# Moving ScalarE's copies for the degree table behind 16 more groups of gathers in a graph-network kernel

## The chip, the cores and the metric

The kernel runs on one core of one Trainium2 chip. The metric is device microseconds of one launch, as the median of several runs. Beside the runs there is one profiled execution, whose time and span are given below. Start times in the trace are microseconds from the start of the span.

## The reference

The inputs are x (100,000 nodes x 128 features), 25,000 edges (src, dst), and edge_attr (25,000 x 64). What is computed:

```
h = relu(layernorm(x))
two layers of:  fwd = segment_mean(h[src] over dst); bwd = segment_mean(h[dst] over src)
                h = concat(h, fwd, bwd) @ W + b        (relu after the first layer only)
x = x + h
h = relu(layernorm(x))
agg = segment_sum(edge_attr over dst)
x = x + MLP(concat(h, agg, u[0]))                      (256 -> 256 -> 256 -> 128, leaky relu)
```

The segment means divide by the degrees of the nodes (how often a node stands in dst, or in src, and at least 1). The part of the kernel around the change prepares those degrees.

## The kernel before

The edges are worked on in G = 98 groups of 256. Each group has 512 edge ends (4 slots of 128 partitions). Each engine has a program of its own; they meet only at semaphores, and within an engine the order is that of the text. The program has these parts, one after the other:

- **The first stage.** Two jobs run side by side. The first is the *picks*: for each group g, ScalarE writes two index columns (`pick_at`, L748) and issues the zero fill of a later piece of `sums1` (512 KB, L741, only up to g = 93); GpSimd then issues two indirect gathers of rows of x into `picked` (L589); SyncE stores `picked` to `xdst` (L376). `picked` and `pick_at` have four buffers each. The second is the *count* of degrees: VectorE writes one-hot rows (`onehot_lo` L980, `onehot_hi` L981, 392 instructions of each), and TensorE multiplies them (L1301, two matmuls for each pair of one-hots) into four banks of PSUM. The two jobs share no data.
- **The degree table.** When the count has ended, VectorE copies the banks to `degree` (L1099), TensorE transposes them (L1392) and signals `s_degT` twice. ScalarE then copies the banks to the high half of `table` (`degree_table()`, L756 and L757, twice) and signals `s_tablehi`; VectorE writes the low half (L1104, L1106) and signals `s_table`. TensorE waits for `s_table` before everything of layer 1: `spread_keys` (L1338), `look_up` (28 matmuls, L1319), `degrees` (L1330), the transposes (L1346) and products (L1355, L1361).
- **The first two groups of layer 1.** VectorE's program goes on, after the table, with `upper_digits(1)`, `lower_digits(0)` (L1043, needs the look-up), `repeated(0)` (L1052 to L1060), `end_stats` and `negated` of groups 0 and 1 (L996, L1005, L1010), `scales(0)`. ScalarE's side of this is `first_group()`: `centre(0)`, `centre(1)` (L685, L691), `transposed(0)` (L701), `messages(0)` (L711), `dense_rows(0)` (L722).
- **The loop of layer 1** over the groups. Its scatters into `sums1` (L579, four for each group) are GpSimd's. Then layer 2 and the MLP, which the change doesn't touch.

The order of the picks is the same on SyncE, GpSimd and ScalarE. It is written in `picks(eng, pick, early, late, last)`: groups 0 to 3; a loop over groups 4 to 59; `early()`; a loop over 60 to 75; `late()`; a loop over 76 to 91; `last()`; groups 92 to 97. With `early`, SyncE and GpSimd load the first two groups of layer 1 (`first_loads`, `first_ends`). With `last`, SyncE loads and GpSimd gathers group 2, and ScalarE does `first_group()`. Only ScalarE uses `late`:

```
picks(act, pick, nothing, degree_table, first_group)
```

Of the kernel before, what the change touches and what calls it, by code (L numbers as in the profile page):

```python
# [29 lines left out]
def gnn_kernel(nc, x, src, dst, edge_attr, W1, b1, W2, b2, u, w1, b1m, w2, b2m, w3, b3, out):  # L30
# [34 lines left out]
    with ExitStack() as ctx:  # L65
# [217 lines left out]
        def picks(eng, pick, early, late, last):  # L283


            for g in range(4):
                pick(g, g, 1)
            with eng.Fori(1, EARLY) as q:
                for b in range(4):
                    pick(q * 4 + b, b, q + 1)  # L290
            early()
            with eng.Fori(EARLY, LATE) as q:
                for b in range(4):
                    pick(q * 4 + b, b, q + 1)
            late()
            with eng.Fori(LATE, QUADS - 1) as q:
                for b in range(4):
                    pick(q * 4 + b, b, q + 1)
            last()
            for g in range(4 * QUADS - 4, G):  # L300
                pick(g, g % 4, g // 4 + 1)
# [4 lines left out]
        def hold(eng):  # L306


            eng.sem_inc(passed[eng.engine], 1)

        def before(g, n):

            return not isinstance(g, int) or g >= n
# [359 lines left out]
        def _(act):  # L673
# [3 lines left out]
            def layer1():  # L677
                def src_index(g, b):

                    act.activation(index[:, b, 0:2], keys[:, 0, 2:4, bass.ds(g, 1)].rearrange("p s g -> p (s g)"), ACT.Copy)\  # L680
                        .then_inc(b_index, 1)

                def centre(g, b, uses):
                    act.wait_ge(b_moments, g + 1)
                    act.activation(spread[:, b, :], moments[:, b, :, 1], ACT.Sqrt, bias=eps[:, 0:1]).then_inc(b_spread, 1)  # L685
                    act.wait_ge(b_negmean, g + 1)
                    if before(g, 2):

                        act.wait_ge(b_T, g - 1)
                    for s in range(4):  # L690
                        last = act.activation(normed[:, b, s, :], ends[:, b, s, :], ACT.Identity, bias=negmean[:, b, s:s + 1])  # L691
                    last.then_inc(b_centred, 1)
                    if not isinstance(g, int) or g + 2 < G:

                        act.wait_ge(b_src[b], 32 * uses)
                        hold(act)
                        src_index(g + 2, b)

                def transposed(g, b):
                    act.wait_ge(b_T, g + 1)  # L700
                    act.activation(hT[:, b].rearrange("p s f -> p (s f)"), bank[0][:], ACT.Relu).then_inc(b_hT, 1)  # L701

                def messages(g, b):
                    act.wait_ge(b_prod, g + 1)
                    act.wait_ge(b_scale, g + 1)
                    if before(g, 2):

                        act.wait_ge(b_mm, g - 1)
                    hold(act)
                    for s in range(4):  # L710
                        last = act.activation(group_msg[:, b, s, 0:F], bank[1][:, s * P:(s + 1) * P], ACT.Copy,  # L711
                                              scale=endscale[:, b, s:s + 1])
                    last.then_inc(b_msg, 1)

                def dense_rows(g, b, uses):
                    act.wait_ge(b_ymm, g + 1)
                    if before(g, 2):

                        act.wait_ge(b_ykept[b], 16 * (uses - 1))
                    hold(act)  # L720
                    for s in range(4):
                        last = act.activation(end_dense[:, b, (s + 2) % 4, :], bank[5][:, s * P:(s + 1) * P], ACT.Copy,  # L722
                                              scale=rstd[:, b, s:s + 1])
                    last.then_inc(b_yrows, 1)
# [15 lines left out]
                def fill(rows_of, n):  # L740
                    act.dma_start(rows_of.rearrange("(p r) f -> p r f", p=P),  # L741
                                  zeros[:, 0:n * F].rearrange("p (r f) -> p r f", f=F)).then_inc(s_zeroed, 16)
# [10 lines left out]
                def degree_table():  # L753
                    for c in range(2):
                        act.wait_ge(s_degT, c + 1)
                        act.activation(table[:, c, 0, 0:4, :], bank[4 + 2 * c][0:CW, :].rearrange("p (c f) -> p c f", f=P), ACT.Copy)  # L756
                        act.activation(table[:, c, 0, 4:CH, :],  # L757
                                       bank[5 + 2 * c][0:CW, 0:(CH - 4) * P].rearrange("p (c f) -> p c f", f=P), ACT.Copy)\
                            .then_inc(s_tablehi, 1)

                def first_group():
                    centre(0, 0, 1)
                    centre(1, 1, 1)
                    transposed(0, 0)
                    messages(0, 0)
                    dense_rows(0, 0, 1)
# [6 lines left out]
                act.wait_ge(s_eps, 1)  # L773
                for g in range(2):
                    src_index(g, g)
                picks(act, pick, nothing, degree_table, first_group)
                fill(sums1[G * FILL:NR, :], GS // P)
                sweep(act, G // 2, lambda j: [step(j * 2 + b, b, j + 1) for b in range(2)])

            layer1()  # L780
            act.wait_ge(s_bias, 48)

# [831 lines left out]
```

## Time and profile before

| what | value |
|---|---|
| median of 3 runs | 4322.13 us (4296.8, 4322.13, 4326.12) |
| profiled execution, its own time | 4294.77 us |
| its span | 4293.2 us |
| mean granted TensorE clock | 0.944 of full |
| busy share of the span | PE 87%, DVE 74%, POOL 70%, ACT 54% |

The profiled execution's time is 1.6 us over its span. It belongs with the lowest of the three runs, 27 us (0.6%) under their median. The first stage and the entry into layer 1 take the first 440 us or so of the span, and the loop of layer 1 goes on to about 1446 us.

### The profile page before, as it was taken

How to read it: one execution, taken by the hardware profiler on the slowest of the kernel's cores; microseconds unless marked ns; L12 is line 12 of the kernel's file. 1: busy time of each engine (PE TensorE's matmuls, PEld its weight loads, DVE VectorE, ACT ScalarE, POOL GpSimd, SP SyncE). 2: the span in 40 equal slices, each digit the busy share in tenths (PEclk: the TensorE clock that was granted, in tenths of full speed). 3: DMA queues.
4: the chain of work that ended last, by engine and by line, in shares of the span. 5: the costliest groups of instructions: out<-in, count | busy, mean ns of one | idle time of the engine just before them, and what ended most of it. 6: DMA issues, size and time to landing. Idle time of an engine off the chain costs nothing.

```text
span 4293.2 us, 100093 instructions
## 1 busy us (share of the span) xinstructions
PE 3733.9 (87%) x25698; PEld 3280.8 (76%) x25698; DVE 3181.9 (74%) x11005; ACT 2304.9 (54%) x5788; POOL 2999.4 (70%) x2962
## 2 busy tenths in 40 slices
PE   3485899988988688888888888879999999999999
PEld 0123788887888688878788888868888888888888
DVE  2384788888888555556555555569999999999998
ACT  0001444444444455555555555557777777777776
POOL 6614778788888677777777777766666666666665
PEclk6687999999999899999999999989999999999999
DMA  7815777777777577777777777767777777777775
GB/s 277 288 52 169 174 176 176 178 176 176 180 176 180 132 188 190 182 186 190 190 190 190 178 183 189 179 147 158 158 159 157 159 158 158 160 157 158 159 159 123
DMA packets 818323, 742.05 MB, mean 173 GB/s; under 512 B 200444, under 2 KB 629896, under 8 KB 818282
## 3 DMA queue, kind: packets, MB, share of 16 engines
q1 hardware_dynamic: 637702, 522.72, 41.2%
q0 software_dynamic: 166208, 167.10, 26.8%
q10 hardware_dynamic: 14372, 51.75, 3.1%
q8 instruction: 17, 0.28, 0.0%
q14 instruction: 24, 0.20, 0.0%
HBM read 355.07 MB, written 334.83 MB: 161 GB/s over the span
## 4 chain that ended last, share of the span: by engine, by line
PE 40%; DMA 7%; issue 6%; DVE 4%; another core or an unknown queue 3%; ACT 2%; POOL 2%; SPq 2%; ACTq 0%; DVEq 0%; POOLq 0%
PE bank L1559 8%; DMA normed<-in_x_dram 6%; PE bank L1573 4%; PE bank L1572 4%; PE bank L1574 4%; PE bank L1537 2%; PE bank L1530 2%; PE bank L1531 2%; PE bank L1536 2%; PE bank L1532 2%; PE bank L1546 2%; PE bank L1467 2%; DVE stats L1160 2%; PE bank L1468 1%
## 5 line engine op out<-in xcount | busy, mean ns | idle before, releaser
L626 POOL DMA_INDIRECT node<-summed,rep_index x392 | 625.9, 1597 | 229.3 <-issue 147.8
L579 POOL DMA_INDIRECT sums<-summed,rep_index x392 | 620.4, 1583 | 156.5 <-issue 130.2
L657 POOL TENSOR_TENSOR resid<-node_out,b3s 128x128 f32<-128x128 f32 x784 | 336.4, 460 | 478.1 <-DVE rows L1281 475.3
L1231 DVE SCALAR_TENSOR_TENSOR z<-bank,bias,small 128x512 f32<-128x512 f32 x784 | 567.7, 744 | 68.3 <-ACT small L889 59.2
L889 ACT ACTIVATE small<-bank,bias_small 128x512 f32<-128x512 f32 x784 | 535.0, 683 | 107.1 <-PE bank L1574 59.5
L667 POOL TENSOR_TENSOR z_lo<-z,z_hi 128x512 fp32r<-128x512 f32 x392 | 496.5, 1288 | 10.2 <-ACT z_hi L920 10.2
L611 POOL DMA_INDIRECT ends<-sums,index x392 | 381.8, 974 | 121.7 <-issue 120.2
L1467 PE MATMUL bank<-hx,W1s 128*128 128x128 f32 x1568 | 324.9, 291 | 159.8 <-ACT hx L830 151.7
L1467 PEld LDWEIGHTS bank<-hx,W1s 128*128 128x128 f32 x1568 | 251.2, 201 | 193.1 <-issue 192.8
L1559 PE MATMUL bank<-w3s,z 128*128 128x128 f32 x3136 | 382.4, 275 | 3.1 <-DVE z L1231 3.1
L1559 PEld LDWEIGHTS bank<-w3s,z 128*128 128x128 f32 x3136 | 365.7, 192 | 4.0 <-DVE z L1231 4.0
L589 POOL DMA_INDIRECT picked<-in_x_dram,pick_at x196 | 188.1, 960 | 216.2 <-ACT pick_at L748 128.0
L1319 PE MATMUL bank<-upper,table 112*128 112x256 bf16 x2744 | 322.3, 276 | 16.8 <-DVE upper L1035 8.7
L820 ACT ACTIVATE resid<-normed,shift,rstd 128x128 f32<-128x128 f32 x784 | 323.1, 498 | 1.6 <-DVE shift L1176 1.1
L809 ACT ACTIVATE spread<-moments,eps 128x4 f32<-128x4 f32 x196 | 58.2, 297 | 494.9 <-DVE moments L1165 245.6
L1301 PE MATMUL bank<-onehot_hi,onehot_lo 128*128 128x392 bf16 x784 | 196.7, 382 | 144.8 <-issue 82.7
L1572 PE MATMUL bank<-z_hi,w_hi 128*128 128x512 f32 x784 | 322.1, 411 | 0.0
L1468 PE MATMUL bank<-ident,rows 128*128 128x128 f32 x1568 | 318.3, 286 | 0.0
L1319 PEld LDWEIGHTS bank<-upper,table 112*128 112x128 bf16 x2744 | 267.7, 99 | 55.7 <-DVE upper L1035 13.3
L1444 PE MATMUL bank<-group_msg,same 128*128 128x192 f32 (+1 forms) x1960 | 308.7, 313 | 0.0
L1573 PE MATMUL bank<-z_lo,w_hi 128*128 128x512 f32 x784 | 306.1, 390 | 0.0
L1574 PE MATMUL bank<-z_hi,w_lo 128*128 128x512 f32 x784 | 305.8, 390 | 0.0
(152 smaller groups left out, 9762.6 us busy)
## 6 DMA issues: line engine op xcount, KB each, us to landing
node<-blank SPq DMA_DIRECT2D x98, 768.0 KB
sums<-zeros ACTq DMA_DIRECT2D x98, 512.0 KB
normed<-in_x_dram SPq DMA_DIRECT2D x196, 256.0 KB
rows<-sums SPq DMA_DIRECT2D x196, 256.0 KB
y<-node_out SPq DMA_DIRECT2D x196, 256.0 KB
node_out<-node SPq DMA_DIRECT2D x196, 256.0 KB, 3.2
node_out<-y POOLq DMA_DIRECT2D x196, 256.0 KB, 4.2
a_parts<-a_pair SPq DMA_DIRECT2D x784, 64.0 KB, 2.5
```

The source lines that it names most:

```text
L579: pool.indirect_dma_start(sums1, bass.IndirectOffsetOnAxis(ap=rep_index[:, b, s:s + 1], axis=0), summed[:, b, s, 0:F], None, compute_op=AL ...
L611: pool.indirect_dma_start(ends[:, b, s, :], None, sums1, bass.IndirectOffsetOnAxis(ap=index[:, b, s:s + 1], axis=0))\
L626: pool.indirect_dma_start(node1, bass.IndirectOffsetOnAxis(ap=rep_index[:, b, s:s + 1], axis=0), summed[:, b, s, :], None, compute_op=ALU. ...
L667: pool.tensor_tensor(z1_lo[:, st.b % 2, m, :], z1[:, st.b % 2, m, :], z1_hi[:, st.b % 2, m, :].bitcast(F32), ALU.subtract).then_inc(e_z1lo, 1)
L889: act.activation(small[:, m, :], bank[first_bank + m][:], ACT.Identity, scale=SLOPE, bias=bias_small[:, m:m + 1]).then_inc(ready, 1)
L1231: dve.scalar_tensor_tensor(out=z[:, m, :], in0=bank[first_bank + m][:], scalar=bias[:, m:m + 1], in1=small[:, m, :], op0=ALU.add, op1=ALU. ...
L1319: last = pe.matmul(bank[2][:, c * EG:(c + 1) * EG], table[:, c, i, r, :], upper[:, b, r, c * EG:(c + 1) * EG], start=(r + i == 0), stop=(r ...
L1467: pe.matmul(o, W1s[:, 0, :], hx[:, i, s, :], start=True, stop=False)
L1559: last = pe.matmul(bank[4][:, s * P:(s + 1) * P], z2[:, c, s * P:(s + 1) * P], w3s[:, c, :], start=(c == 0), stop=(c == HB - 1))
L1572: pe.matmul(bank[2 + m][:], w2_hi[:, c, cols], z1_hi[:, d, c, :], start=(c == 0), stop=False)
L1573: pe.matmul(bank[2 + m][:], w2_hi[:, c, cols], z1_lo[:, d, c, :], start=False, stop=False)
L1574: last = pe.matmul(bank[2 + m][:], w2_lo[:, c, cols], z1_hi[:, d, c, :], start=False, stop=(c == HB - 1))
```

## The change

`degree_table()` is taken from the place `late`, behind group 75, and put at the head of `first_group()`, behind group 91. Nothing else is touched, on any engine.

```
                 def first_group():
+                    degree_table()
                     centre(0, 0, 1)
                     centre(1, 1, 1)
                     transposed(0, 0)
...
-                picks(act, pick, nothing, degree_table, first_group)
+                picks(act, pick, nothing, nothing, first_group)
```

`degree_table()` is two waits and four instructions:

```
for c in range(2):
    act.wait_ge(s_degT, c + 1)
    act.activation(table[:, c, 0, 0:4, :], bank[4 + 2 * c]...)
    act.activation(table[:, c, 0, 4:CH, :], bank[5 + 2 * c]...).then_inc(s_tablehi, 1)
```

## Rows read from the trace of the kernel before

**Rows 1.** The page, busy tenths of GpSimd in 40 slices of 107 us.
```profile
POOL 6614778788888677777777777766666666666665
```

**Rows 2.** Busy time in stretches: PE, PEld, DVE, ACT, POOL, TensorE clock, DMA share, GB/s.
```profile
14.00:238.00 224.00, 85.91 (x272) 25.75 (x272) 69.70 (x264) 14.72 (x72) 148.93 (x156) 0.62 0.78 277
238.00:349.50 111.50, 110.78 (x512) 30.40 (x512) 110.11 (x512) 0.00 (x0) 0.00 (x0) 0.98 0.01 3
349.50:398.00 48.50, 17.51 (x89) 12.69 (x89) 17.28 (x62) 9.74 (x34) 30.44 (x32) 0.60 0.71 251
```

**Rows 3.** The same view for line L981 alone, VectorE's `onehot_hi`.
```profile
20.00:40.00 20.00, 5.94 (x19) 0.88 0.86 322
40.00:60.00 20.00, 1.89 (x6) 0.50 0.72 251
...
20.00:238.00 218.00, 45.28 (x132) 0.61 0.78 275
238.00:349.50 111.50, 84.46 (x256) 0.98 0.01 3
```

**Rows 4.** The same view for line L589 alone, GpSimd's pick gathers.
```profile
20.00:238.00 218.00, 138.90 (x145) 0.61 0.78 275
...
349.50:398.00 48.50, 30.44 (x32) 0.60 0.71 251
```

**Rows 5.** Timeline of ScalarE: start, us, what, and the idle time before it.
```profile
351.67 0.60 ACT L756 ACTIVATE table<-bank 112x512 bf16<-112x512 f32 x1 [122.11 <-PE bank L1392]
...
392.00 1.28 ACT L685 ACT_TABLE_LOAD   x1 [0.46 <-issue]
...
396.21 0.57 ACT L701 ACTIVATE hT<-bank 128x512 f32<-128x512 f32 x1
402.50 1.14 ACT L711 ACTIVATE group_msg<-bank,endscale 128x128 f32<-128x128 f32 x4 [5.71 <-remote]
...
404.02 0.67 ACT L722 ACTIVATE end_dense<-bank,rstd 128x128 f32<-128x128 f32 x2
```

**Rows 6.** Timeline of GpSimd.
```profile
236.38 0.95 POOL L589 DMA_INDIRECT picked<-in_x_dram,pick_at  x1 [0.30 <-issue]
354.48 0.95 POOL L589 DMA_INDIRECT picked<-in_x_dram,pick_at  x1 [117.15 <-ACT pick_at L748]
...
405.57 0.95 POOL L589 DMA_INDIRECT picked<-in_x_dram,pick_at  x1 [5.28 <-issue]
...
423.18 1.63 POOL L579 DMA_INDIRECT sums<-summed,rep_index  x1 [0.31 <-issue]
```

**Rows 7.** Timeline of VectorE.
```profile
69.67 0.29 DVE L980 TENSOR_SCALAR onehot_lo<-iota_lo,hilo 128x256 bf16<-128x256 f16 x1 [4.39 <-remote]
...
364.42 0.75 DVE L1043 SCALAR_TENSOR_TENSOR lower<-hilo_all,digits,bank 128x512 f32<-128x512 f16 x1 [6.11 <-remote]
...
368.67 0.87 DVE L996 BATCH_NORM_STATS2 stats<-ends 128x6 f32<-128x128 f32 x4
...
379.95 0.17 DVE L1010 TENSOR_SCALAR negmean<-moments 128x4 f32<-128x4 f32 x1 [0.96 <-DVE moments L1005]
...
407.07 0.87 DVE L996 BATCH_NORM_STATS2 stats<-ends 128x6 f32<-128x128 f32 x4 [11.79 <-DMA ends<-xdst]
...
408.54 0.17 DVE L1010 TENSOR_SCALAR negmean<-moments 128x4 f32<-128x4 f32 x1
...
434.08 0.75 DVE L1043 SCALAR_TENSOR_TENSOR lower<-hilo_all,digits,bank 128x512 f32<-128x512 f16 x1 [18.57 <-remote]
```

**Rows 8.** Timeline of TensorE.
```profile
348.76 0.76 PE L1301 MATMUL bank<-onehot_hi,onehot_lo 128*128 128x392 bf16 x3
...
355.78 4.89 PE L1319 MATMUL bank<-upper,table 112*128 112x256 bf16 x28
...
396.84 2.08 PE L1355 MATMUL bank<-W1s,hT 128*128 128x128 f32 x8 [0.91 <-issue]
```

**Rows 9.** Line L579, GpSimd's scatters of layer 1: shortest, median, longest ns, first and last start.
```profile
L579 POOL DMA_INDIRECT sums<-summed,rep_index x392: 1550/1577/1680, 423.2 to 1444.4; - x196
```

More of the change, by code:

```diff
@@ L761, in first_group @@
                 def first_group():
+                    degree_table()
                     centre(0, 0, 1)
@@ L775, in layer1 @@
                     src_index(g, g)
-                picks(act, pick, nothing, degree_table, first_group)
+                picks(act, pick, nothing, nothing, first_group)
                 fill(sums1[G * FILL:NR, :], GS // P)
```

## The prediction

> **What bounds the kernel now.** I read the page's slices first: GpSimd is 6 tenths busy in slices 1 and 2, 1 tenth in slice 3 (215 to 322 us), and busy again from slice 4 on [rows 1]. So something in the first stage stops the picks. The timelines say what: ScalarE stood for 122.1 us until TensorE's transposes of the degrees, and GpSimd for 117.2 us until ScalarE's next `pick_at` [rows 5, 6]. The last gather before the stop ends at 237.3 and the next starts at 354.5. ScalarE was at `degree_table()` with nothing to copy, and the 16 groups of picks behind it had no need of the table. Read so far, the change looks like 40 us for nothing.
>
> The view by stretches is the one that decides. The reader is to compare its first two rows [rows 2]. While the picks run (14 to 238 us), DMA is 78% busy, the granted clock averages 0.62 of full, and VectorE and TensorE, which only count and share no data with the picks, are busy 31% and 38% of the time. When the picks have stopped (238 to 349.5), DMA is at 1%, the clock at 0.98, and both are busy 99%. The same for `onehot_hi` alone: 132 in 218 us beside the picks, 0.606 each us; 256 in 111.5 us without them, one each 0.4355 us, 2.296 each us [rows 3]. So the stall of GpSimd is time in which the count runs at nearly four times its speed. The end of the count (349.5, the last matmuls of L1301 [rows 8]) releases the table, the table releases the entry into layer 1, and the loop of layer 1 then runs to 1446 us, paced by its own work: its 392 scatters start over 1021 us, 10.4 us a group [rows 9], of which four of 1.58 us and the 0.3 us behind each are 7.5, and GpSimd's two gathers of group rows come on top. No idle time waits there to take up a later or earlier start. So the price of the change is by how much the point is moved at which that loop gets going; everything behind it moves along.
>
> **The change, part by part.** I measure at the end of `dense_rows(0)`, the last instruction of `first_group()`, 404.02 + 0.67 = 404.7 [rows 5], which is 55.2 us behind the end of the count. Behind it the programs of both kernels are the same. It is (end of the count) + (chain from there).
>
> *1. The four copies themselves.* The same four instructions, some 0.6 us each at most [rows 5], leave one place and enter another. They release VectorE directly in both. Cost 0.
>
> *2. What the copies no longer hold up: 16 groups of picks.* These are 16 `pick_at`, 16 zero fills of 512 KB, 32 gathers on GpSimd and 16 stores on SyncE. They now run from 237 us on, where the stall stood. Gathers of groups up to 75 came 145 in 218 us, 3.01 us a group [rows 4], so the 16 groups take 48.1 us at that pace; behind the count they took from 354.5 to about 397.8, or 43 us, 32 gathers [rows 4, 6]. I take 48.1, since it is the pace beside a running count, and keep 43 as the other end. The picks end at some 285 us, far ahead of the count's end, so ScalarE reaches `degree_table()` with 100 us to spare and the table isn't made late by its new place. SyncE's and GpSimd's `last` steps get a free queue.
>
> *3. What that costs the count.* In 48.1 us beside picks VectorE writes 48.1 x 0.606 = 29.1 of `onehot_hi`, which alone take 29.1 x 0.4355 = 12.7 us. The count ends 48.1 - 12.7 = 35.4 us later, at 384.9. With 43 us of picks it is 26.1 counted, 11.4 us saved, 31.7 later. Single stretches of 20 us beside picks held 6 to 19 of `onehot_hi` [rows 3], so over 48 us, where such stretches partly even out, I allow 31 to 40 us. The bounds from further off: 48 us, if the count stood altogether, and 0, if the picks weren't what slowed it.
>
> *4. The chain from the end of the count to `dense_rows(0)`.* In the kernel before it shares the DMAs with the 16 groups and ScalarE serves it only behind them: `centre(0)` starts, with a table load, at 392.0, 0.5 us behind the last `pick_at` of group 91, although `negmean` of group 1 had been ready since 380.1 [rows 5, 7]. On the way VectorE waits 6.1 us for `lower`, which starts 3.7 us behind the last matmul of the look-up (355.78 + 4.89 = 360.7) [rows 7, 8]. Without picks I add up: end of the count to the start of the look-up 6.3 (349.5 to 355.8); the look-up 4.9; from `lower` to `stats` 4.25 (364.42 to 368.67); `stats` to the end of `negmean` twice, 2 x 1.64 (407.07 to 408.71); the second `centre` behind it 1.5 (392.0 to 396.2 held the load of 1.3 and two of them); `hT` 0.6; its products 2.1 and the second half of them as much; `dense_rows` 1.2 [rows 5, 7, 8]. That is 26.2, and 27.2 with hand-overs of 0.1 us or so each. ScalarE's table load of 1.28 us before the first square root finds room while VectorE does group 1. Against the 55.2 of before the chain gains 28.0 us. The other end: if the waits inside the chain stay (380.1 - 349.5 = 30.6 to `negmean`, then 12.7 from 392.0 to 404.7 less the first centre, 1.4), it is 42, and gains 13. I take 27.2, for those waits stood in the stretch with DMA at 0.71, and rows 2 show VectorE without gaps where DMA is idle.
>
> *5. Behind `dense_rows(0)`.* Groups 92 to 97 are picked, GpSimd issues 12 gathers and two more from 405.57 and then the first scatter at 423.18 [rows 6]; VectorE's `lower` of group 2 waits 18.6 us until 434.1 [rows 7], and the loop is at speed from about 440. The same traffic meets the same steps in both kernels, only the backlog of groups 88 to 91 is gone. I take 2 us for it; bounds are 0 and 10 us of gain (the part of the 18.6 us that lies behind GpSimd's queue).
>
> *The sum:* + 35.4 - 28.0 - 2 = + 5.4 us. Against the profiled execution 4294.8 becomes 4300.2; against the median of the runs, 4322.1, it is 4327.5. The profiled execution stands with the lowest run, and runs of the same kernel lie up to 29 us apart, five times the effect. About 1% (43 us) is what a measurement of this kernel can tell from no change.
>
> **A rule of the Trainium skill.** VectorE waited 4.4 us ahead of a one-hot (69.67 us) while single gathers take 0.95 us on GpSimd [rows 6, 7]. The Trainium skill, "SBUF — State Buffer", says that VectorE in a two-port mode and GpSimd take a shared pair of ports by an exclusive lock, held for one instruction. By that rule the count would lose only GpSimd's busy time, 32 x 0.95 = 30.4 us, and the sum would be + 0.4 us instead of + 5.4. The trace speaks against it as the whole cause, as the wait is longer than several such instructions and 0.3 us lie free between them.
>
> **The rivals.**
>
> *A. The count isn't slowed by picks* (it was slow by its own start, with TensorE's clock at the lower level). Then item 3 is 0, and the time is 4322.1 - 28 - 2 = 4292. For it: the granted clock in the first stretch is 0.62 [rows 2]. Against it: VectorE is idle two thirds of it too, and the full rate stands from 238.0, 0.7 us behind the last gather's end, not from a point of the count's own. Chance 0.06.
>
> *B. The picks cost the count less than the average.* 43 us of picks, 19 of `onehot_hi` in each 20 us (the best stretch), the 10 us behind: 43 - 17.8 = 25 us later, - 28 - 10 = - 13, 4309. The port rule above goes this way too, with + 0.4. Chance 0.12 for gains of 6 to 20 us.
>
> *C. The chain doesn't shorten.* The waits of VectorE and ScalarE between the count and `dense_rows(0)` belong to their entering new code and not to the traffic. Place: `lower` and `negmean` on VectorE, `group_msg` on ScalarE. Then the chain is 42 and the sum 35.4 - 13 - 2 = + 20, 4342; with the count standing still beside the picks, + 33, 4355. It decides from a chain of some 34 us behind the count on, where the sum passes + 12. For it: they are marked as ended by an unknown queue. Against: in the stretch without DMA no such wait stands. Chance 0.14.
>
> *D. The change does nothing* (ScalarE would stand elsewhere for the same 122 us, and the picks with it): the program's order excludes it, since nothing between groups 76 and 91 needs the table. Below 0.01.
>
> **How the numbers follow.** The forecast, - 6 to + 15 us about + 5, has 0.67; A 0.06; B 0.12; C 0.14; D and the rest 0.01. The range takes in B and C and the spread of the runs: the low end is 4297 (the lowest run) + 5 - 13 = 4289, the high end 4326 + 20 = 4346. Faster by over 1% would need under 4279: only A together with low runs, 0.02. Slower by over 1% is over 4365: C with a count that stands still and high runs, 0.03. Within 1%: 0.95.
>
> **What would show it.** In the profile of the changed kernel: GpSimd's gathers run on without a gap from 237 to about 285 us; `onehot_hi` there some 29 in 48 us with the clock near 0.6; the last L1301 at 385 and not at 349.5; ScalarE's wait ahead of `table` about 100 us, now behind group 91; from the last count matmul to `lower` 12 us rather than 15, to the end of `dense_rows(0)` 27 rather than 55; first scatter at some 427 to 430 rather than 423.2; scatters still 10.4 us a group. I'm wrong if the count's end stays below 370 (then A or B) or if the chain behind it is over 34 us (C).

## The result

| kernel | runs | median | lowest to highest |
|---|---|---|---|
| before | 12 | 4318.75 us | 4282.96 to 4336.83 |
| changed | 12 | 4322.24 us | 4253.59 to 4326.57 |

The changed kernel's runs fall into two groups with nothing between them: five at 4253.59, 4262.65, 4263.43, 4265.45 and 4269.83, and seven from 4322.10 to 4326.57. The ratio 0.9879 [0.9842, 0.9916] counts the upper seven as slow runs and leaves them out; the changed kernel's profile on another chip (a_again, below) runs as I forecast and speaks for their being the kernel itself (forecast 4327.5), though no run of this upper group was profiled. The lower group is something that I hadn't forecast. The profiled execution, 4262.65 us with a span of 4261.0, is of the lower group.

The page of the changed kernel has GpSimd's slices, for [rows 1]: the hole of slice 3 is gone, a shallow one of 311 to 345 us is left in slice 4.
```profile
POOL 6674877887777677777777777766666666666665
```
The view by stretches, for [rows 2]: PE, PEld, DVE, ACT, POOL busy, granted clock, DMA share, GB/s.
```profile
180.00:200.00 20.00, 4.18 (x10) 0.66 (x10) 2.52 (x9) 1.02 (x5) 15.60 (x17) 0.50 0.57 191
217.00:311.00 94.00, 93.97 (x441) 24.96 (x440) 94.00 (x441) 4.91 (x24) 77.26 (x55) 1.00 0.61 210
```
This is the reading that decides. The second row can't be had by mixing rows 2 of before: GpSimd is 82% busy with picks, DMA is at 0.61, and VectorE and TensorE are 100% busy with the clock at 1.00. In the row above it, which ends 17 us earlier, the same two jobs share the chip at the old price: 9 VectorE instructions in 20 us. The same view for `onehot_hi` alone (now L982, since lines behind the added one moved by one), for [rows 3]:
```profile
20.00:238.00 218.00, 59.19 (x181) 0.65 0.74 261
238.00:290.00 52.00, 37.40 (x123) 1.00 0.66 228
```
Where I had forecast 0.606 each us beside the picks of groups 76 to 91, it was 123 / 52 = 2.37. From here on I call such a way for the two jobs to share the chip, with its own pair of rates, a regime: slow for 0.6 of `onehot_hi` each us, fast for 2.3 and more. The timeline of GpSimd shows where the one gives way to the other, for [rows 6]:
```profile
200.51 0.95 POOL L589 DMA_INDIRECT picked<-in_x_dram,pick_at  x1 [0.30 <-issue]
215.84 1.11 POOL L589 DMA_INDIRECT picked<-in_x_dram,pick_at  x1 [14.38 <-DMA xdst<-picked]
...
309.57 1.41 POOL L589 DMA_INDIRECT picked<-in_x_dram,pick_at  x1 [0.30 <-issue]
...
369.23 1.63 POOL L579 DMA_INDIRECT sums<-summed,rep_index  x1 [0.30 <-issue]
```
At about 201 us GpSimd waits 14.38 us for a store of `picked`, which stands on SyncE's queue behind `first_loads` (group 60, `early`). Up to there a gather takes 0.95 us, behind it 1.41. The gathers go on without a stop from 237 us, as forecast, but to 311 and not to 285. The timelines of TensorE, VectorE and ScalarE give the chain, for [rows 5, 7, 8]:
```profile
321.69 5.46 PE L1302 MATMUL bank<-onehot_hi,onehot_lo 128*128 128x392 bf16 x25
...
333.42 3.22 PE L1320 MATMUL bank<-upper,table 112*128 112x256 bf16 x28
```
```profile
336.68 0.75 DVE L1044 SCALAR_TENSOR_TENSOR lower<-hilo_all,digits,bank 128x512 f32<-128x512 f16 x1 [0.99 <-PE bank L1320]
...
343.89 0.17 DVE L1011 TENSOR_SCALAR negmean<-moments 128x4 f32<-128x4 f32 x1
...
380.37 0.75 DVE L1044 SCALAR_TENSOR_TENSOR lower<-hilo_all,digits,bank 128x512 f32<-128x512 f16 x1 [22.03 <-remote]
```
```profile
329.30 0.60 ACT L756 ACTIVATE table<-bank 112x512 bf16<-112x512 f32 x1 [28.92 <-PE bank L1393]
...
331.24 1.28 ACT L685 ACT_TABLE_LOAD   x1
...
348.22 1.14 ACT L711 ACTIVATE group_msg<-bank,endscale 128x128 f32<-128x128 f32 x4 [2.28 <-PE bank L1356]
...
350.38 0.38 ACT L722 ACTIVATE end_dense<-bank,rstd 128x128 f32<-128x128 f32 x1
```
The count ends at 321.69 + 5.46 = 327.15 (before: 349.52), 22.4 us earlier, and `dense_rows(0)` at 350.76 (404.7), 53.9 us earlier. From the one to the other it is 23.6 us instead of 55.2. The first scatter follows 18.5 us behind, as in before: 369.2 instead of 423.2.

Grouped rows of the scatters of layer 1 and, in the second, of layer 2 (shortest, median, longest ns, first and last start), for [rows 9]:
```profile
L579 POOL DMA_INDIRECT sums<-summed,rep_index x392: 1549/1577/1690, 369.2 to 1397.9; - x196
L626 POOL DMA_INDIRECT node<-summed,rep_index x392: 1549/1577/2141, 1430.3 to 2772.1; - x196
```
The kernel before, the second of them:
```profile
L626 POOL DMA_INDIRECT node<-summed,rep_index x392: 1550/1577/2161, 1477.7 to 2803.2; - x196
```
So 54.0 us at the first scatter, 46.5 at the last, 31.1 at the end of layer 2, and 32.2 in the span. It looks like a gain given back. It isn't shown to be one: see "The rest of the span" below.

### The profile page after: what moved, and what is told of

It is laid out like the page before. It is cut to its first block, busy times and chain, and to the rows that moved or that the text cites. A ratio compares the mean times of both kernels' runs of the same rounds, so it can differ in the third digit from the quotient of the medians.

```text
span 4261.0 us, 100093 instructions
## 1 busy us (share of the span) xinstructions
PE 3726.9 (87%) x25698; PEld 3278.0 (77%) x25698; DVE 3177.7 (75%) x11005; ACT 2305.6 (54%) x5788; POOL 3023.1 (71%) x2962
## 4 chain that ended last, share of the span: by engine, by line
PE 41%; issue 7%; DMA 6%; DVE 4%; another core or an unknown queue 4%; ACT 3%; SPq 1%; POOL 1%; ACTq 0%; DVEq 0%; POOLq 0%
PE bank L1560 8%; DMA normed<-in_x_dram 5%; PE bank L1574 4%; PE bank L1573 4%; PE bank L1575 4%; PE bank L1538 2%; PE bank L1531 2%; PE bank L1532 2%; PE bank L1537 2%; PE bank L1533 2%; PE bank L1547 2%; DVE stats L1161 2%; PE bank L1468 2%; PE bank L1469 1%
## 5 line engine op out<-in xcount | busy, mean ns | idle before, releaser
L579 POOL DMA_INDIRECT sums<-summed,rep_index x392 | 620.0, 1582 | 164.6 <-issue 131.1
L1445 PEld LDWEIGHTS bank<-group_msg,same 128*128 128x128 f32 x1960 | 299.6, 192 | 0.0
```

The source lines that it names most:

```text
L579: pool.indirect_dma_start(sums1, bass.IndirectOffsetOnAxis(ap=rep_index[:, b, s:s + 1], axis=0), summed[:, b, s, 0:F], None, compute_op=AL ...
L1445: last = pe.matmul(o, same[:, b, j, i * P:(i + 1) * P], group_msg[:, b, j, 0:w], start=(j == 0), stop=(j == i))
```

## The experiments

Four sets ran, each on another chip. The kernel before took 4051.2, 4286.6, 4317.5 and 4316.3 us on them (medians of 13, 23, 15 and 13 runs), so every kernel is compared with before on its own chip. e1, e2, e3, e5 and e6 are edits of the changed kernel, e4 is one of the kernel before; a is the changed kernel and b the kernel before, without an edit.

| run | chip of | median (runs) | before there | ratio | last matmul of the count starts | first scatter |
|---|---|---|---|---|---|---|
| e1_loads_last | set 1 | 4072.57 (8) | 4051.22 | 1.0079 [1.0052, 1.0106] | 201.1 | 310.7 |
| e2_fills_after | set 1 | 4180.10 (2) | 4051.22 | 1.0320 [1.0295, 1.0345] | 190.5 | 414.9 |
| e3_head_start | set 1 | 4117.41 (5) | 4051.22 | 1.0163 [1.0149, 1.0178] | 187.5 | 358.6 |
| e4_head_start_late | set 1 | 4103.35 (4) | 4051.22 | 1.0133 [1.0115, 1.0151] | 188.8 | 343.0 |
| a_again | set 2 | 4292.34 (12) | 4286.58 | 0.9983 [0.9945, 1.0022] | 383.8 | 426.3 |
| b_again | set 2 | 4283.05 (8) | 4286.58 | 0.9997 [0.9963, 1.0031] | 352.9 | 426.5 |
| e5_one_port | set 2 | 4371.83 (2) | 4286.58 | 1.0196 [1.0112, 1.0280] | 272.2 | 537.9 |
| e1_again | set 3 | 4323.45 (10) | 4317.45 | 1.0006 [0.9987, 1.0025] | 387.4 | 431.7 |
| e2_again | set 3 | 4440.93 (1) | 4317.45 | one run | 399.3 | 567.2 |
| e3_again | set 3 | 4347.70 (4) | 4317.45 | 1.0069 [1.0043, 1.0095] | 187.8 | 455.6 |
| e4_again | set 3 | 4295.83 (6) | 4317.45 | 0.9856 [0.9822, 0.9891] for its lower three | 187.2 | 450.1 |
| a_third | set 4 | 4315.74 (10) | 4316.34 | 0.9981 [0.9947, 1.0015] | 329.7 | 374.9 |
| b_third | set 4 | 4323.23 (1) | 4316.34 | one run | 357.3 | 435.4 |
| e6_psum_rows | set 4 | 4429.58 (2) | 4316.34 | 1.0270 [1.0230, 1.0310] | 501.4 | 545.0 |

The theories, as the expectations name them: R, the regime changes by itself, whatever the loads do; Q, the DMA queues are overfull while the count is slow, and a pause in them lets the count get to speed; P, VectorE and GpSimd share a way to memory, and who has it keeps it; T, turns of about 0.7 us that hold instruction streams while GpSimd gathers, whatever the one-hot looks like.

**Set 1: four edits, on a chip where nothing of this stands in the way.** The first moves the loads of groups 0 and 1 from `early` to `last`, so that no pause falls among the picks:
```
-picks(sp, pick, first_loads, nothing, lambda: loads(2, 0, 2))
+picks(sp, pick, nothing, nothing, lambda: (first_loads(), loads(2, 0, 2)))
-picks(pool, pick, first_ends, nothing, lambda: gather_src(2, 0))
+picks(pool, pick, nothing, nothing, lambda: (first_ends(), gather_src(2, 0)))
```


> The changed kernel, with the loads for the first two groups of layer 1 (first_loads on SyncE, first_ends on GpSimd) moved from behind group 59 to behind group 91, so that nothing pauses the picks in the middle. Theory Q (two regimes: the count runs slowly while the picks keep the DMA queues overfull, and a pause of the picks of 14 us lets it change to full speed, which it then keeps beside the picks): without the pause no change of regime; onehot_hi stays near 0.6 each us until the picks end at some 285 us, the count ends at some 385, the first scatter starts at some 430, median within 10 us of 4322. Theory R (the full speed beside picks comes from the change itself or from the time since the start, not from the pause): the count again runs at 2.3 each us from some 210 us on and ends near 328, time near 4262.

The second takes the zero fills out of the picks, behind the whole first stage:
```
-if not isinstance(g, int) or g + 4 < G:
-    fill(sums1[bass.ds((g + 4) * FILL, FILL), :], FILL // P)
...
 picks(act, pick, nothing, nothing, first_group)
+with act.Fori(4, G) as g:
+    fill(sums1[bass.ds(g * FILL, FILL), :], FILL // P)
```


> The changed kernel with the zero fills of groups 4 to 97 (512 KB each) taken out of the picks and issued in one loop behind the last pick; GpSimd's first scatter waits for all of them, so the whole gets longer by 100 to 160 us. Only the first 330 us of its profile are of interest. Theory Q (DMA queues overfull): with some 512 KB of 900 KB a group gone, the count runs at 2.3 onehot_hi each us beside the picks from the start and ends at 185 to 200 us; gathers take 1.40 us each until then, 0.95 behind it. Theory P (the port shared by VectorE and GpSimd alone): the gathers are still there, 0.95 us long, and the count stays at some 0.6 each us beside them.

The third lets the count run alone until 48 of its matmul pairs are done, and the fourth does the same to the kernel before:
```
+pool.wait_ge(s_count, 48)
 picks(pool, pick, first_ends, nothing, lambda: gather_src(2, 0))
```


> The changed kernel, with GpSimd's first pick gather held back until the first 48 of 392 count steps are done (some 22 us of picks lost), so that the picks meet a count that already runs at full speed with TensorE's clock up. Theory Q: the fast regime holds from the start: gathers 1.40 us, 3.4 us a group, onehot_hi 2.3 each us, count ended at 185 to 200 us; the picks of group 91 end at 310 to 330, then the table and its chain of 21 to 27 us; first scatter at 355 to 380; all runs close together, at 4245 to 4275. Theory R: the count falls to 0.6 each us as soon as gathers start, and all is 10 to 20 us later than in the changed kernel, two groups of times as there.

> The same head start of 48 count steps in the kernel before, whose table copies stand behind group 75. Theory Q: the count has ended (at 185 to 200 us) before ScalarE comes to the copies (at 260 to 280 us), so neither ScalarE nor the picks wait there, the chain behind the table runs beside the last picks, first_group() follows the pick of group 91 at 310 to 330 at once; first scatter at 335 to 355, 15 to 25 us ahead of the head start in the changed kernel; time 4225 to 4260. Theory R: as the kernel before, 10 to 20 us later.

These runs tell little between the theories, because on this chip the count was never slow. By stretches, e1_loads_last:
```profile
40.00:180.00 140.00, 136.92 (x606) 34.34 (x606) 140.00 (x607) 10.43 (x51) 109.37 (x101) 1.00 0.81 282
```
DMA is at 0.81, higher than in [rows 2], GpSimd is 78% busy with gathers, and VectorE has no gap. The count is over at 201 us, when the picks are still running. Copies at their old place don't stop the picks on such a chip: in e4_head_start_late ScalarE reached them at 272.98 us and waited 0.47 us. What these runs show is the price of the edits where there is nothing to win. Against before it is 21 us for e1, 129 for e2 and 66 for e3, each together with the move of the copies, since the changed kernel itself didn't run on this chip, and 52 for e4, which has the head start alone. The pair e3 and e4 differs by the move alone: with it the kernel is 14 us slower (4117.41 against 4103.35, first scatter 358.6 against 343.0). In this pair, where the count is over early, the move costs. That the same kernel before takes 4051 us here and 4287 to 4318 on the other three chips is the largest difference of this study, and it isn't explained.

**Set 2: the two kernels again.** No edit.

> The changed kernel once more. On a chip where the kernel before takes some 4050 us, theory Q: the count is over before either place of the copies, so nothing is freed by the move, and the chain of table, look-up and statistics (21 us in the first profile after, 26.2 added up in the prediction) now lies behind the pick of group 91 instead of beside the picks: 10 to 25 us slower than before, ratio 1.003 to 1.006. On a chip where before takes some 4300 us: two groups of times, 4253 to 4270 and 4322 to 4327. Theory R: the move saves the 33 to 54 us of the first pair of profiles on either chip, ratio 0.987 to 0.992.

> The kernel before once more, for its profile beside runs of the other chip. On a chip where the kernel before takes some 4050 us, theory Q says that the count runs at full speed beside the picks from the start (2.2 onehot_hi each us), ends at some 200 us, and that ScalarE therefore doesn't wait at the copies behind group 75: first scatter at 290 to 300. On a chip where it takes some 4300 us: a stop of the picks of 60 to 120 us there, first scatter at 370 to 425. Theory R (nothing differs but the later parts): the stop is there on either chip.

The changed kernel, a_again, its 12 runs: one at 4231.82 and the others from 4279.60 to 4308.50, so all but one lie together, and the one some 48 us under them. Its profiled execution (4288.08) shows what I had forecast. `onehot_hi` by stretches, the last three at the pause of the picks behind group 59:
```profile
20.00:238.00 218.00, 43.73 (x135) 0.61 0.75 269
238.00:286.00 48.00, 9.92 (x30) 0.57 0.75 268
290.00:380.00 90.00, 66.19 (x209) 1.00 0.02 6
205.00:208.00 3.00, 2.02 (x7) 0.50 1.07 382
208.00:215.00 7.00, 4.88 (x16) 1.00 0.54 196
216.00:236.00 20.00, 1.61 (x5) 0.56 0.71 257
```
Its timelines of GpSimd, TensorE and ScalarE:
```profile
210.62 0.95 POOL L589 DMA_INDIRECT picked<-in_x_dram,pick_at  x1 [8.64 <-DMA xdst<-picked]
...
375.70 8.45 PE L1302 MATMUL bank<-onehot_hi,onehot_lo 128*128 128x392 bf16 x39
...
386.31 0.60 ACT L756 ACTIVATE table<-bank 112x512 bf16<-112x512 f32 x1 [103.01 <-PE bank L1393]
...
407.37 0.38 ACT L722 ACTIVATE end_dense<-bank,rstd 128x128 f32<-128x128 f32 x1
```
30 of `onehot_hi` in 48 us of picks (forecast 29.1), the count's end at 384.15 (384.9), ScalarE's wait 103 us (about 100), the chain 407.75 - 384.15 = 23.6 us (27.2), and the first scatter at 426.3 (427 to 430). Against before on the same chip, whose count ended at 353.27, that is 30.9 us later, at the lower end of my 31 to 40.

The pause at `early` was shorter here, 8.64 us, and the gathers behind it kept their 0.95 to 1.02 us. The three rows at the pause show two things more. The count was at full speed from 205 us on, and for 3 us of it the granted clock was still 0.50: so a lower clock of TensorE isn't what makes the slow regime slow. And it stayed at full speed for some 4 us beside the first gathers, with the clock at 1.00, and then fell to 5 of `onehot_hi` in 20 us. To be at full speed when the gathers come isn't enough to stay there. The kernel before on this chip, ScalarE's timeline:
```profile
355.42 0.60 ACT L756 ACTIVATE table<-bank 112x512 bf16<-112x512 f32 x1 [123.04 <-PE bank L1392]
```
and its first scatter at 426.5: the later count and the shorter chain cancel to 0.2 us. I had expected a stop of 60 to 120 us and a first scatter at 370 to 425 here; both came out a little above.

**Set 2: one-hots with another way of reading.** Each iota value is stored twice and read with step 2, so that VectorE might give up its fast form of reading:
```
-pool.iota(iota_hi[:], pattern=[[1, HALF]], ...)
+pool.iota(iota_hi[:], pattern=[[1, HALF], [0, 2]], ...)
...
-dve.tensor_scalar(onehot_hi[:, s, :], iota_hi[:], ...)
+dve.tensor_scalar(onehot_hi[:, s, :], iota_hi[:].rearrange("p (n t) -> p n t", t=2)[:, :, 0], ...)
```
(`iota_lo` likewise.)

> The changed kernel with the counting rows iota_lo and iota_hi stored with a step of 2 elements, so that VectorE's one-hots read with a step and run at one element a cycle: some 0.33 and 0.47 us in place of 0.20 and 0.23 from start to start, 0.8 us a pair, 310 us of count. Theory P (gathers and one-hots contend for what the fast form of the one-hots uses): gathers stay at 0.95 us throughout, and no waits of several us ahead of the one-hots anywhere; count ended at 325 to 345 us. Theory Q (DMA queues overfull, sequencers wait): on a chip of 4300 us the waits of 0.7 us and their multiples stay, with the count still at 0.6 each us beside the picks; on a chip of 4050 us no such waits in either case, and the gathers alone tell about the port (0.95 against 1.08 to 1.41).

The edit didn't do what it was for: a pair of one-hots takes 0.59 us from start to start (0.26 and 0.34), where I had expected 0.8 and the unedited pair takes 0.43. So this run doesn't test P. But its trace holds the clearest row of all. GpSimd:
```profile
53.20 219.59 POOL L589 DMA_INDIRECT picked<-in_x_dram,pick_at  x1 [6.14 <-ACT pick_at L748]
```
VectorE in the middle of it:
```profile
200.39 0.34 DVE L981 TENSOR_SCALAR onehot_lo<-iota_lo,hilo 128x256 bf16<-128x256 f16 x1
200.65 0.41 DVE L982 TENSOR_SCALAR onehot_hi<-iota_hi,hilo 128x392 bf16<-128x392 f16 x1
```
One gather of a usual 0.95 us took 219.59 us, and 368 pairs of one-hots without a gap ran beside it; the last of them ends at 271.97 and the gather at 272.79. So GpSimd can be kept out for as long as the one-hots come. No long pause stood ahead of it: the wait before this gather is 6.14 us, shorter than the one in a_again. Both of its runs were slower than before's median (4399.28 and 4344.39); whether by 2% or less is unclear.

**Set 3: the edits of set 1 where the count is slow.**

> The changed kernel with first_loads and first_ends moved behind group 91, once more, for a chip on which the kernel before takes some 4300 us. Theory Q (the count changes to full speed only if the picks pause long enough): as there is no pause, the profile shows 0.6 onehot_hi each us to some 285 us, a count ended at some 385 and a first scatter at 426 to 432; all runs in the upper group of the changed kernel's times, none 40 us under it. Theory R (the change of regime comes by itself): some runs 40 to 60 us under the others. On a chip of 4050 us: as in the first run, 4061 to 4102.

Without the loads at group 60 the count stayed slow until the picks ended. `onehot_hi` by stretches:
```profile
200.00:286.00 86.00, 15.81 (x49) 0.58 0.73 255
290.00:380.00 90.00, 79.94 (x202) 0.95 0.09 28
```
From 30 to 290 us GpSimd's longest wait is 4.12 us. The first scatter came at 431.7, and the ten runs lie between 4305.94 and 4327.72: no lower group. That is as Q expected and speaks against R, by which the regime would have changed without the pause, but weakly: where 8 runs in 34 of the unedited kernel lie low (below), ten without one come about 1 time in 15 by chance, and that kernel wasn't run on this chip.

> The changed kernel with the zero fills of groups 4 to 97 behind the last pick, once more, for a chip of 4300 us; the whole is 60 to 140 us longer, only the first 300 us count. Theory Q (DMA queues overfull): count at 2.3 onehot_hi each us from the start beside the gathers, ended at 185 to 200 us. Theory P (port alone): 0.6 each us beside the gathers.

By stretches, all engines:
```profile
20.00:200.00 180.00, 53.50 (x151) 11.22 (x148) 38.77 (x147) 12.47 (x61) 121.48 (x128) 0.55 0.35 103
```
The fills are gone and DMA is at 0.35 instead of 0.78, and yet VectorE is 22% busy, less than in [rows 2]. The theory of the overfull queues falls with this row, and with e1_loads_last from the other side (DMA at 0.81, count at full speed). What is left beside the count is the gathers, 128 in these 180 us. So they alone can bring the slow regime on such a chip, though on the chip of set 1 they don't.

> The changed kernel with the head start of 48 count steps, once more, for a chip of 4300 us. Theory Q: regime of full speed from the start and kept, as in the run on the other chip: gathers of 1.40 us, count ended at some 190 us, first scatter at 355 to 365; time 4225 to 4245, that is 65 us less the 10 us or so of GpSimd's later parts, under the upper group of the changed kernel's times. Theory R: the count falls to 0.6 each us when the gathers start, first scatter at 430 to 450.

> The kernel before with the head start of 48 count steps, once more, for a chip of 4300 us. Theory Q: first scatter at 343 as on the other chip, so 80 us ahead of the kernel before (423 to 426): 4200 to 4225, ratio 0.980 to 0.984 where the kernel before takes 4287. On a chip of 4050 us: again 50 us slower than before. Theory R: slower than before on either chip.

With a head start of 48 pairs the count kept full speed on this chip too, to its end at 188 us, and GpSimd paid: the first scatter came at 455.6 and 450.1, where 355 to 365 and 343 were expected, and e3_again took 4347.70 us and not 4225 to 4245. The gathers weren't at 1.40 us. e3_again by stretches, and its GpSimd:
```profile
40.00:180.00 140.00, 139.94 (x654) 37.11 (x654) 140.00 (x655) 2.46 (x12) 130.83 (x26) 1.00 0.19 68
```
```profile
41.56 26.00 POOL L589 DMA_INDIRECT picked<-in_x_dram,pick_at  x1 [34.55 <-PE bank L1303]
67.86 6.53 POOL L589 DMA_INDIRECT picked<-in_x_dram,pick_at  x1 [0.30 <-issue]
```
26 gathers in 140 us, 5 us each, the first 26.00 and the later ones down to some 3. The same kernel on the chip of set 1, the same stretch:
```profile
40.00:180.00 140.00, 139.94 (x656) 37.09 (x654) 140.00 (x656) 7.98 (x39) 113.58 (x81) 1.00 0.63 219
```
81 gathers of 1.4 us beside the same count. So three regimes exist, not one, and one kernel can meet more than one of them. The head start in the kernel before (e4_again) ran 4254.33, 4256.71 and 4259.94 in three runs and 4331.73, 4344.33 and 4354.37 in three. The ratio in the table describes the lower three alone. The profiled one (4331.73) is of the upper three, with gathers of up to 26 us; no trace of a lower one was taken.

**Set 4: once more, and one-hots that read from PSUM.**

> The changed kernel once more. On a chip of 4050 us (count fast beside the picks from the start): 10 to 25 us slower than before. On a chip of 4300 us: like before within 5 us, first scatter at 426 to 430, but single runs 40 to 60 us under the rest.

> The kernel before once more. On a chip of 4050 us: no stop of the picks at the copies, first scatter at 285 to 300. On a chip of 4300 us: stop of 115 to 125 us, first scatter at 423 to 427.

The changed kernel ran 4261.28 and 4265.81 in two runs and 4304.50 to 4329.71 in eight. The profiled one is of the lower two. Its GpSimd:
```profile
201.21 0.95 POOL L589 DMA_INDIRECT picked<-in_x_dram,pick_at  x1 [0.30 <-issue]
218.92 1.32 POOL L589 DMA_INDIRECT picked<-in_x_dram,pick_at  x1 [16.76 <-DMA xdst<-picked]
220.54 1.40 POOL L589 DMA_INDIRECT picked<-in_x_dram,pick_at  x1 [0.30 <-issue]
```
Its `onehot_hi`:
```profile
20.00:200.00 180.00, 32.06 (x99) 0.60 0.75 266
220.00:300.00 80.00, 58.05 (x188) 1.00 0.64 219
```
It is the picture of the first profile again: a pause of 16.76 us at the same place, 0.55 of `onehot_hi` each us ahead of it, 2.35 behind it, gathers 0.95 and then 1.40 us. First scatter 374.9, against 435.4 in the kernel before on this chip (b_third, a single run, whose picks stopped for 123.42 us, as expected, but whose first scatter was expected at 423 to 427).

The other edit copies the two iotas into PSUM first:
```
+dve.tensor_copy(bank[4][:, 0:HALF], iota_hi[:])
+dve.tensor_copy(bank[5][:, 0:2 * P], iota_lo[:])
...
-dve.tensor_scalar(onehot_hi[:, s, :], iota_hi[:], ...)
+dve.tensor_scalar(onehot_hi[:, s, :], bank[4][:, 0:HALF], ...)
```


> The changed kernel with the counting rows held as f32 in two banks of PSUM, so that the one-hots read PSUM and take one element a cycle: some 0.9 to 1.0 us a pair in place of 0.43, a count of 350 to 390 us if it never waits. Theory P (port): no waits of several us ahead of one-hots on any chip; gathers at 0.95 us throughout; count ended at 370 to 410 us, picks of group 91 ended by 290. Theory T (turns of 0.70 us that the sequencers of SyncE, ScalarE and VectorE take while GpSimd gathers, whatever the form of the one-hot): on a chip of 4300 us the waits of 3 to 5 us stay, some 0.6 or fewer one-hots each us until the picks end at 285, count ended at 470 to 500 us.

By stretches, beside the picks ahead of the pause at `early`, behind that pause, and without picks; then VectorE's timeline and GpSimd's first gather behind the pause:
```profile
40.00:180.00 140.00, 65.03 (x168) 10.71 (x168) 79.94 (x168) 9.66 (x48) 90.13 (x95) 0.56 0.75 266
220.00:300.00 80.00, 42.29 (x102) 6.67 (x102) 47.71 (x101) 4.91 (x24) 52.30 (x55) 0.50 0.70 243
300.00:420.00 120.00, 101.20 (x255) 16.41 (x254) 117.99 (x256) 0.00 (x0) 1.17 (x2) 0.56 0.01 4
```
```profile
113.25 0.48 DVE L984 TENSOR_SCALAR onehot_lo<-bank,hilo 128x256 bf16<-128x256 f32 x1 [4.67 <-issue]
...
118.17 0.48 DVE L984 TENSOR_SCALAR onehot_lo<-bank,hilo 128x256 bf16<-128x256 f32 x1 [3.91 <-remote]
```
```profile
220.61 0.95 POOL L589 DMA_INDIRECT picked<-in_x_dram,pick_at  x1 [16.92 <-DMA xdst<-picked]
```
These one-hots take 0.92 us a pair alone, so the kernel is slower by their length. Beside picks there are 84 of `onehot_hi` in 140 us, 0.60 each us, against 128 in 120 us or 1.07 alone. The 0.60 is the rate of before beside picks, though each one-hot is twice as long: in the slow regime the pace of the count isn't set by the length of its instructions. The waits of 3.9 and 4.7 us ahead of a one-hot are still there, and the gathers kept 0.95 us. P would have the waits gone; it is at most part of the cause. T had expected the waits, some 0.6 each us and a count ended at 470 to 500 us; its last matmul starts at 501.4. And behind the longest of all the pauses at `early`, 16.92 us, this count stayed slow (51 of `onehot_hi` in 80 us, 0.64 each us): with PSUM as the source the pause didn't bring the fast regime, in the one profile that there is.

## Why the prediction was right and wrong

**Item 1, the copies themselves at 0: right.** The same four copies follow each other from 329.30 us on, and the first takes 0.60 us as before.

**Item 2, 16 groups of picks run where the stop stood: right in place.** In the slow regime they end near 286 us (forecast 285); in the profile of the changed kernel they take 1.41 + 0.30 us a gather and end at 311.

**Item 3, "in 48.1 us beside picks VectorE writes 48.1 x 0.606": the step that failed.** In a_again, 30 in 48 us and an end 30.9 us behind that of before on its chip bear the arithmetic out, if from the low side. What failed is that I took 0.606 for a property of the pair of jobs. It is the rate of one regime. In the two profiles of lower runs the rate was 2.37 and 2.35 from 217 or 220 us on, beside running picks, and in the first of them the count ended 22.4 us earlier than before and not 35.4 later: 57.8 us off, on the term that I had bounded from 0 to 48. My bounds only knew a count that loses something to the picks of groups 76 to 91. They left out that it could already run faster beside groups 60 to 75. I had read that "the full rate stands from 238.0, 0.7 us behind the last gather's end" as what the picks cost; it also shows what a pause does, and the change lets the picks go on behind a pause.

**What brings the other regime.** Three things are shown, all on chips whose plain kernels are slow. After a head start of 48 matmul pairs the count stays at full speed to its end (e3_again and e4_again, 40 to 180 us), though with gathers of 3 to 26 us. Without a pause the slow count stays slow as long as the gathers come (e1_again, 200 to 286). And in both profiles with a change of regime it stands at GpSimd's long wait behind `first_loads`, 14.38 and 16.76 us; with waits of 8.64 (a_again), 7.64 (b_again), 4.85 (e2_again) and 3.31 us (before, at 204.55) the count was at full speed in the wait or just behind it, and fell back within some us of the next gathers. That the length of this wait decides is an inference from these profiles, and not a rule: in e5_one_port one-hots kept GpSimd out behind a wait of 6.14 us, and in e6_psum_rows, with another source of the one-hots, 16.92 us changed nothing. e1_again, without the wait, has no lower group in ten runs on a chip where the unedited changed kernel didn't run. No edit lengthened the pause in the changed kernel, which would be the test. The wait itself differs from run to run for a reason that no run shows.

**Item 4, the chain of 27.2 us: right, a little too long.** 23.6 us in the first profile and in a_again, with and without the change of regime. `lower` waits 0.99 us instead of 6.1, and the table load lies at 331.24, ahead of need. The look-up took 3.22 us and not 4.89. Rival C (0.14) falls.

**Item 5, 2 us behind it: nothing.** 369.23 - 350.76 = 18.5 us, before 423.18 - 404.7 = 18.5. `lower` of group 2 still waits, 22.03 us.

**The sum.** Forecast + 35.4 - 28.0 - 2 = + 5.4. In a_again, by the first scatter against before on the same chip: 426.3 - 426.5 = - 0.2, which is + 30.9 for the table's start (386.31 against 355.42) and - 31.1 behind it. In the first profile: - 22.4 - 31.6 = - 54.0; on the chip of set 4, 374.9 - 435.4 = - 60.5.

**The rest of the span.** From the first scatter to the end of the span, the first profile has 3891.8 us and before 3870.0, and that is where 22 of the 54 us went. On one chip the two kernels agree: 4286.5 - 426.3 = 3860.2 and 4283.4 - 426.5 = 3856.9 in set 2, 3889.3 and 3886.2 in set 4, where the span is 57.4 us shorter with an entry 60.5 us earlier. The medians say the same: the five lower runs have 4263.43, 55 us under before's 4318.75. So "everything behind it moves along" held, to some 3 us, and the 22 us belong to the two profiled executions and not to the change. Why they differ is open.

**Rivals and chances.** A (4292) and B (4309) had the sign of the lower runs right, but neither gives the size: in A the count loses nothing, in B less than I forecast, and in neither does it gain. A's reason, the lower clock of TensorE, isn't it either: in a_again the count was at full speed for 3 us at a clock of 0.50. I gave 0.95 to within 1% and 0.02 to faster. Of all runs of the changed kernel, 8 of 34 lie more than 1% under the median of before on their chip (5 of 12, 1 of 12, 2 of 10), and the medians over all runs differ by 3.5, 5.8 and 0.6 us. The change comes to 1.3% in the lower runs, whose count got going in both that were profiled, and to nothing in the others. My range ended at 4289, above all of the lower runs. That end was also added up wrongly: it puts B's - 13 on top of the forecast's + 5, though - 13 was already the whole sum of B, which gives 4297 - 13 = 4284, still above them.

**Is there a better version?** Not one that holds. Of the six runs of the head start in the kernel before (e4_again) three are some 60 us under before's median and three are slower than its slowest run (4330.11), and it costs 52 us on the chip of set 1. The changed kernel as it stands wasn't run on that chip; by the pair e3 and e4 the move costs 14 us there beside a head start.

## What to carry to other kernels

A rate read from a stretch where two jobs overlap is the rate of a state, not of the pair: before using it as a price, look for any stretch of the trace in which the same two jobs overlap at another rate, and ask what pauses the edit removes or leaves in front of the overlap. Work that starts again behind a pause meets an engine that is already at speed, and may leave it there or pull it down again, as both happened here. And when the runs of one kernel fall into two groups, profile both before believing a ratio that keeps one of them.

## What the runs showed of the hardware

**VectorE and GpSimd beside each other have three regimes.** Gathers 0.95 us and one-hots at a quarter of their speed; gathers 1.40 us (1.08 in e1_loads_last) and one-hots at full speed; one-hots at full speed and gathers of 3 to 26, once 219.59 us. The Trainium skill, "SBUF — State Buffer" (Who interferes with whom), has the pair of ports that GpSimd and a VectorE in a two-port mode both use as an exclusive lock held for one instruction, which blocks the other engine. The trace agrees that GpSimd can be blocked: 219.59 us for a gather of 0.95. It goes beyond it in length, as 368 pairs of VectorE instructions ran in that time and not one, and with PSUM as the source VectorE's waits of 3.9 and 4.7 us stay, so the rule doesn't account for the slow regime.

**Instruction streams are held while gathers of 0.95 us run, on every chip but that of set 1.** What is held is not only data. The bookkeeping of registers ahead of an instruction, an entry that touches no data, in before between 100 and 200 us, on VectorE and on ScalarE (shortest, median, longest ns):
```profile
L981 DVEq FUSED_REGOPS  x67: 4/57/711, 101.2 to 199.2; - x67
...
L748 ACTq FUSED_REGOPS  x32: 4/52/1396, 103.3 to 198.0; - x32
```
and in the changed kernel from 217 to 300 us, beside gathers of 1.41 us:
```profile
L982 DVEq FUSED_REGOPS  x195: 53/57/57, 216.9 to 299.7; - x195
...
L748 ACTq FUSED_REGOPS  x23: 52/52/52, 220.2 to 296.4; - x23
```
Beside a count at full speed no such hold is longer than 75 ns, in any profile. But the slow count isn't what they need. In e3_again from 220 to 300 us the count has been over for 30 us, TensorE and VectorE do nothing, and ScalarE's holds are back, beside gathers of 0.95 us:
```profile
L749 ACTq FUSED_REGOPS  x28: 2/52/715, 224.6 to 299.0; - x28
```
The same kernel on the chip of set 1 has none longer than 52 ns on ScalarE there (e3_head_start), beside 56 gathers against 57. Without the fills (e2_again) ScalarE's are gone as well, 57 ns at most, and VectorE's are not, up to 727 ns. So the holds come with the gathers and with the chip: like the slow count itself, they were never seen on the chip of set 1. Why a chip has them, and what the streams of VectorE and ScalarE share with a gathering GpSimd, no run here shows.

**TensorE's clock is mostly at the lower of its levels while its matmuls come with gaps.** It is granted 0.50 to 0.62 of full (1.2 GHz for the most part) in the long slow stretches shown, where TensorE is busy 21 to 38% of the time, and 1.00 (2.4 GHz) beside the same picks once it has no gaps. With the longer one-hots of e6_psum_rows it stays at 0.56 in 120 us without picks, where TensorE is busy 84% of the time and VectorE hardly pauses (98%).
